# Head of a small language-model layer: four chunks' features share one 128-row operand, and a table repeated in four diagonal blocks multiplies it

## What is computed

```
attempts, correct = running counts per (row, skill)          # (32, 512)
f = [skill, attempts, correct / max(attempts, 1), 1]         # four features per token
h = f @ table                       # (32, 512, 64), table is (4, 64)
v = ln(h); scan over 512 steps: x_t = (0.97 x + relu(v Dx^T)) / its L1 norm
           a = rho x_t; y = relu(ln(a) Dy^T) * relu(x_t); out = ln(y E^T)
           rho = 0.97 rho + ln(v) x_t^T
h = h + out; h = h + top-2-of-8 expert MLP(ln(h))
```

## Time and profile before

| | us |
|---|---|
| median of 3 runs (lowest, highest) | 656.93 (656.39, 657.41) |
| the profiled execution | 657.44 |
| its span, first to last instruction | 655.6 |
| groups of the head in it | 62.7 to 107.7 |
| serial stretch behind them | 107.7 to 128.4 |
| turns | 128.4 to the end |

### The profile page before, as it was taken

The page is one execution under the profiler, slowest core; times in us unless marked ns, Lnnn a source line. Parts: engine busy times, 40 slices in busy tenths (PEclk is TensorE's granted clock), DMA queues, the critical chain, the costliest instruction groups (busy, mean ns, idle before and its releaser), DMA issues.

```text
span 655.6 us, 18935 instructions
## 1 busy us (share of the span) xinstructions
PE 609.0 (93%) x5109; PEld 436.1 (67%) x5109; DVE 530.2 (81%) x1890; ACT 426.3 (65%) x1291; POOL 358.0 (55%) x441
## 2 busy tenths in 40 slices
PE   2484998799999999999999999999999999999997
PEld 0363776466677777777777777777777777777744
DVE  4998878765788888888888888888888888888675
ACT  6892776023567766667777667776666677776683
POOL 3001999414365555565666666655666566555654
PEclk9999998899999999999999999999999999999999
DMA  6300000100444444455455544444444444444364
GB/s 198 135 0 1 1 0 1 40 33 33 98 98 108 106 105 109 119 113 117 110 118 109 117 120 120 106 105 105 105 105 105 105 105 105 106 105 106 83 131 98
DMA packets 61623, 60.43 MB, mean 92 GB/s; under 512 B 22124, under 2 KB 57052, under 8 KB 61084
## 3 DMA queue, kind: packets, MB, share of 16 engines
q1 hardware_dynamic: 59164, 59.36, 37.8%
q10 hardware_dynamic: 2240, 0.73, 0.5%
q0 software_dynamic: 192, 0.01, 0.0%
HBM read 55.20 MB, written 4.89 MB: 92 GB/s over the span
## 4 chain that ended last, share of the span: by engine, by line
PE 87%; DVE 8%; issue 2%; ACT 1%; DMA 1%; SPq 0%; POOL 0%; DVEq 0%; ACTq 0%; POOLq 0%
PE bank L1614 16%; PE bank L1472 11%; PE bank L1595 9%; PE bank L1599 8%; PE bank L1537 5%; PE bank L1558 4%; PE bank L1494 3%; PE bank L1508 3%; PE bank L1513 3%; PE bank L1379 2%; PE bank L1483 2%; PE bank L1370 2%; PE bank L1462 2%; PE bank L1332 2%; PE bank L1361 2%
## 5 line engine op out<-in xcount | busy, mean ns | idle before, releaser
L687 ACT ACTIVATE skill_rows<-bank,b1T,w_scale 128x512 f32<-128x512 f32 x256 | 196.1, 778 | 8.4 <-PE bank L1599 6.6
L520 POOL TENSOR_TENSOR feat_parts<-skill_rows 128x512 f32<-128x512 f32 x62 | 79.0, 1275 | 93.8 <-DVE feat_parts L1047 88.9
L1614 PE MATMUL bank<-skill_rows,w_sb 128*64 128x256 f32 x928 | 122.7, 382 | 0.0
L1472 PE MATMUL bank<-feat_parts 128*128 128x128 f32 (+1 forms) x512 | 88.1, 306 | 2.5 <-DVE feat_parts L1030 1.2
L1614 PEld LDWEIGHTS bank<-skill_rows,w_sb 128*64 128x64 f32 x928 | 69.3, 137 | 27.2
L1472 PEld LDWEIGHTS bank<-feat_parts 128*128 128x128 f32 x512 | 78.1, 194 | 11.8 <-DVE feat_parts L1030 1.6
L1047 DVE TENSOR_TENSOR_SCAN feat_parts<-same,feat_parts 128x512 f32<-128x512 f32 x62 | 72.2, 1207 | 0.0
L1148 DVE SCALAR_TENSOR_TENSOR skill_rows<-bank,b2T,skill_rows 128x256 f32<-128x256 f32 x120 | 51.1, 477 | 16.3 <-PE bank L1614 13.4
L711 ACT ACTIVATE bank<-bank 128x64 f32<-128x64 f32 x128 | 26.7, 220 | 50.9 <-PE bank L1567 50.9
L1053 DVE TENSOR_TENSOR feat_parts<-bank,mask_sb 128x128 f32<-128x128 f32 x128 | 36.3, 285 | 28.6 <-PE bank L1472 27.3
L1148 DVE SCALAR_TENSOR_TENSOR skill_rows<-bank,b2T,feat_parts 128x256 f32<-128x256 f32 x112 | 47.6, 478 | 12.6 <-PE bank L1614 11.3
(11 more groups left out here) (284 smaller groups left out, 1506.8 us busy)
## 6 DMA issues: line engine op xcount, KB each, us to landing
skill_rows<-w_d SPq DMA_DIRECT2D x32, 512.0 KB, 6.3
same<-factor_d SPq DMA_DIRECT2D x31, 512.0 KB, 5.5
feat_parts<-w_d SPq DMA_DIRECT2D x30, 512.0 KB, 6.3
skill_rows<-skill_row_d SPq DMA_DIRECT2D x4, 1024.0 KB, 7.8
out<-o_sb SPq DMA_DIRECT2D x28, 128.0 KB, 5.2
feat_parts<-w_d SPq DMA_DIRECT2D x4, 256.0 KB, 4.9
w_sb<-in_L_ffn_W ACTq DMA_DIRECT2D x2, 256.0 KB
w_d<-wT SPq DMA_DIRECT2D x32, 16.0 KB, 1.4
```

Of the source, the lines that this page charges most:

```text
L520: pool.tensor_tensor(half[:, n, :], tm[:, 2 * n, :], tm[:, 2 * n + 1, :], ALU.add).then_inc(po_half, 1)
L687: act.activation(hid[:, e, :], banks[e % len(banks)][:, :], ACT.Gelu, bias=b1T[:, e:e + 1], scale=w1_scale[:, e:e + 1]).then_inc(ac_gelu, 1)
L1472: last = pe.matmul(n_bank[sc % 2][:, 0:SPAN[sc]], xs[:, k, sc * P:(sc + 1) * P], xs[:, k, sc * P:sc * P + SPAN[sc]], start=(k == 0), stop= ...
L1614: last = pe.matmul(z_bank[q % 2][n * D:(n + 1) * D, at:at + S // 2], w2_sb[:, e, :], hid[:, e, n * (S // 2):(n + 1) * (S // 2)], start=Tru ...
```

## The change

The features now take SLOTS = 8 columns for a piece (4 whole, 2 middle, 2 low) and ROWS = 32 columns for a chunk, so that four chunks fill 128. One transpose gives `feat_k` the rows of four chunks. `table_k` has four diagonal blocks: block c holds the table in rows 32c to 32c+23 and zeros elsewhere. A group is 2 transposes, 2 products of 256 columns and 4 of 512 columns. The zeros, the copies and the transposed features shrink with it; `table_k`, its clearing by VectorE before the counting, and the table's transfers on SyncE's queue (10 before, 13 now) grow.

Banks 2 and 4 are read by ScalarE now, 3 and 5 by VectorE (before 2 and 3, 4 and 5). `h` of even groups is copied by ScalarE, of odd groups by VectorE.

`update(b, k)` has to give each chunk its own weights: four products of 128 columns in place of one of 512.

On GpSimd the quadratic form is written with operations that multiply and add in one, with scalars by partition, in 19 steps up to `rstd` where there were 24 (the first, `gram_two`, on 20 columns in both). The power for `u_scale` is cut in two: 8 columns (rows of tokens 0 and 1) before `weighted_input(0)`, 120 behind it, and the mean comes before both.

```diff
-KF = NF * PIECES * PIECES
+SLOTS = 8
+ROWS = P // C
...
-        table_k = sb("table_k", [P, D + NS], BF16)
+        table_k = sb("table_k", [P, C, D + NS], BF16)
...
+        slots = parts_flat[:, 0:J * ROWS].rearrange("p (j n) -> p j n", n=ROWS)
...
+            for c in range(C):
+                sp.dma_start(table_k[c * ROWS:c * ROWS + PIECES * SLOTS, c, :], table_d.rearrange("g s n -> (g s) n"))\
+                  .then_inc(ld_table, 16)
...
+                def more(total, f, scalar):
+                    step(pool.tensor_scalar(t, f, scalar, None, ALU.mult))
+                    step(pool.tensor_tensor(total, total, t, ALU.add))
...
+                step(pool.tensor_scalar(a, skill, one(0, 0), two(0, 3), ALU.mult, ALU.add))
+                more(a, tries, two(0, 1))
+                more(a, ratio, two(0, 2))
+                step(pool.tensor_tensor(a, a, skill, ALU.mult))
...
             moments()
+            input_scales(0, 2)
             weighted_input(0)
+            input_scales(2, B)
+            pool.wait_ge(scales_in, 2)
...
             def group(g, side):
-                act.wait_ge(pe_h0, g + 1)
-                act.activation(h_all[:, bass.ds(g * GROUP * D, GROUP * D)], h0_bank[side][:, :], ACT.Copy)\
-                   .then_inc(h0_in, 1)
-                for n in range(HALF):
+                if side == 0:
+                    act.wait_ge(pe_h0, g + 1)
+                    act.activation(h_all[:, bass.ds(g * GROUP * D, GROUP * D)], h0_bank[side][:, :], ACT.Copy)\
+                       .then_inc(h0_a, 1)
+                for n in range(0, PAIRS, 2):
...
-                dve.tensor_copy(feat_k[:, bass.ds(g * GROUP * P, GROUP * P)], feat_bank[side][:, :].bitcast(BF16))\
+                dve.tensor_copy(feat_k[:, bass.ds(g * 2 * P, 2 * P)], feat_bank[side][:, :].bitcast(BF16)[:, 0:2 * P])\
                    .then_inc(featT_in, 1)
...
+                if side == 1:
+                    dve.wait_ge(pe_h0, g + 1)
+                    dve.tensor_copy(h_all[:, bass.ds(g * GROUP * D, GROUP * D)], h0_bank[side][:, :]).then_inc(h0_v, 1)
+                for n in range(1, PAIRS, 2):
...
-            def group(g, side):
+            def group(g, side, pair):
                 pe.wait_ge(featT_in, g + 1)
-                wait(pe, h0_in, g - 1)
-                for n in range(GROUP):
-                    last = pe.matmul(h0_bank[side][:, n * D:(n + 1) * D], feat_k[:, bass.ds((g * GROUP + n) * P, P)],
-                                     table_k[:, 0:D], start=True, stop=True)
+                wait(pe, (h0_a, h0_v)[side], pair)
+                for n in range(2):
+                    last = pe.matmul(h0_bank[side][:, n * C * D:(n + 1) * C * D].rearrange("p (c d) -> p c d", c=C),
+                                     feat_k[:, bass.ds((2 * g + n) * P, P)], table_k[:, :, 0:D], start=True, stop=True)
                 last.then_inc(pe_h0, 1)
...
             def update(b, k):
 
                 wait(pe, dv_y, 2 * NK * b + NK * (k - 1))
-                pe.matmul(n_bank[k][:, :], table_k[:, D + k * P:D + (k + 1) * P],
-                          feat_k[:, bass.ds(b * S, S)], start=True, stop=True).then_inc(pe_pre, 1)
+                for c in range(C):
+                    last = pe.matmul(n_bank[k][:, c * P:(c + 1) * P], table_k[:, c, D + k * P:D + (k + 1) * P],
+                                     feat_k[:, bass.ds(b * P, P)], start=True, stop=True)
+                last.then_inc(pe_pre, 1)
```

More of the change, by code:

```diff
@@ L432, in _ @@
             pool.wait_ge(rows_set, 3)
-            def each(row, i, j):
-                at = i * (NF + 1) + j
-                return row[:, at:at + 1].to_broadcast([P, J])
             def moments():
                 k = Steps(pool, form_steps)
-                f, t = [feat[:, i, :] for i in range(NF)], form[:, 3, :]
-                def step(out, a, b, how):
-                    k.done(pool.tensor_tensor(out, a, b, how))
+                skill, tries, ratio, ok = [feat[:, i, :] for i in range(NF)]
@@ L458, in moments @@
[L458 to L464, removed]
-                pool.tensor_tensor(rstd[:], rstd[:], power_j[:], ALU.pow).then_inc(rstd_in, 1)
@@ L466, in moments @@
[L466 to L471, removed]
+                step(pool.tensor_tensor(gram_two[:], gram_row[:], gram_row[:], ALU.add))
@@ new lines, in moments @@
+                step(pool.tensor_scalar(b, ratio, one(2, 2), two(2, 3), ALU.mult, ALU.add))
+                step(pool.tensor_tensor(b, b, ratio, ALU.mult))
+                step(pool.tensor_tensor(a, a, b, ALU.add))
+                more(a, ok, one(3, 3))
+                step(pool.tensor_scalar(var_h0[:], a, 0.0, None, ALU.max))
+                step(pool.tensor_scalar(rstd[:], var_h0[:], EPS, DECAY * DECAY, ALU.add, ALU.mult))
+                pool.tensor_tensor(rstd[:], rstd[:], power_j[:], ALU.pow).then_inc(rstd_in, 1)
@@ L472, in moments @@
                     .then_inc(scales_in, 1)
[L473 to L476, removed]
             def weighted_input(b):
@@ L1372, in group @@
                 last.then_inc(pe_h0, 1)
                 for n in range(PAIRS):
-                    read = 2 * HALF * (g - 1) + 2 * (n % HALF) + 2
                     if not isinstance(g, int) or g > 0:
-                        pe.wait_ge(sum_a if n < HALF else sum_v, read)
-                    for k in range(2):
-                        last = pe.matmul(bank[2 + n][:, k * NS:(k + 1) * NS],
-                                         feat_k[:, bass.ds((g * GROUP + 2 * n + k) * P, P)],
-                                         table_k[:, D:D + NS], start=True, stop=True)
@@ L1412, in keep_running @@
                 for _ in range(n):
-                    pe.matmul(idle_bank[:, :], table_k[:, D:D + P], feat_k[:, 0:S], start=True, stop=True)
+                    pe.matmul(idle_bank[:, :], table_k[:, 0, D:D + P], feat_k[:, 0:S], start=True, stop=True)
             keep_running(2, bank[1])
```

104 lines of the change are left out of this document (61 added, 43 removed).

## The result

| | before | with the change |
|---|---|---|
| median (lowest to highest), 4 runs each | 656.66 us (655.71 to 657.41) | 645.50 us (645.01 to 646.25) |
| ratio of the times, 95% interval | | 0.9834 [0.9815, 0.9852] |
| profiled execution; its span | 657.44; 655.6 us | 645.01; 643.2 us |

The kernel is 11.2 us faster by the medians. In the tables here the span is cut at four marks: the first transpose of the head's groups, VectorE's product of `upd_sum` with `rstd`, the first product with `skill_rows,first` behind the scans, and the first transpose of the turns.

A forecast was written before the change was run, and what follows sets the result against it. TensorE's instruction count was taken to bound the head's groups, and TensorE to fill the main loop. -10.5 (groups) and +0.6 (updates) gave -9.9: 647.0 us against the 656.93 median, range 644.5 to 653.5.

The forecast's parts named there:

- The bound of before: Head's groups: TensorE sets the pace by its count of instructions, with an address row ahead of each, not by columns.
- The groups: Head's groups: VectorE becomes the bound at 4.0 us for two groups; stage ends at 97.2 instead of 107.7, -10.5 us.
- The two unknown copies: VectorE in the head's groups: feature copy of 256 columns taken as 0.25 less 0.05 overlap, copy of `h` as 0.55 us.
- bounds for the stage: VectorE's sums and copies in the head's groups: 31.5 us expected, 30.9 to 37.5 with the bounds of both copies.
- Ahead of the groups: Before the head's groups: clearing `table_k` +0.40 us, two shorter copies of feature columns -0.37 for both.
- The serial stretch: Scans and products behind the head's groups: instructions unchanged, no sum; low-clock parts may fall elsewhere, +-1 us.
- The updates: 64 updates, each four products of 128 columns for one of 512: 0.01 us more each, +0.6 us.
- The rival by which they would cost more: Updates: weight loads only half hidden, 5.1 instead of 0.6 us, 651.5; by the skill's page 653.1; chance 0.08.
- it does not hold `rstd`: GpSimd beside the head's groups: `rstd`'s power starts at 72.5, ends at 93.3, 3.9 us ahead of VectorE.
- 5 us of cover: GpSimd before the turns: second power done at 120.3, `ub` of row 1 wanted at 125.6.
- The lower clock: Rival, head's groups: TensorE at 1.2 GHz needs 4.7 us for two groups, 5.6 more, 652.6; chance 0.07.
- The slower case: Rival, loop of turns: each piece of an update pays 0.14 us, 18 us over 52 updates, 665; chance 0.05.

## Why the prediction was right

The forecast was -9.9 us. The medians give -11.2, the two profiles -12.5 between their spans. Part of both is luck with the clock: all four runs of the change had a mean granted clock of 0.995, while 20 of the 39 later runs of the kernel before had 0.992 or less. At equal clock, over all runs of the two kernels on all chips, the change gives 10.0 us (655.66 and 645.70 at 0.995, 11 and 7 runs) and 10.5 (657.10 and 646.56 at 0.992, 18 and 2 runs). So the sum was nearer than the medians show.

**The bound of before.** The loop's rows for each product, not its columns, set TensorE's pace: shown by the loop written out, whose products are the same and take 0.40 for 1.14 us.

**The groups: forecast -10.5, measured -10.9** (and -10.7 in the second profile of the change). VectorE is the bound, 3.98 us for two groups against a forecast of 4.0, and ScalarE stands close behind it, with 0.2 to 0.35 us of waiting in two groups. The two unknown copies, in the groups by line and shape:

```profile
L951 DVE COPY h_all<-bank 128x512 f32 x6 | 4.1, 684 | 0.0
L945 DVE COPY feat_k<-bank 128x256 bf16 x12 | 3.5, 289 | 0.0
```

The copy of `h` has 684 ns; the row that gave the upper bound had 683. It starts 0.59 us ahead of its neighbour (78.37 to 78.96); forecast 0.55. The copy of 256 columns has 289 ns, 0.21 from start to start; forecast 0.20. The start of the stage, 2.27 us to VectorE's first sum, was forecast as 2.16. The row for the stretch says clock 1.00, but four products of 512 columns take 1.71 us in the chain of the first group and 0.90 in a later one: half the clock at first, as the forecast had it from the earlier trace rows. The forecast's bounds for the stage, "30.9 to 37.5", do not follow from its own terms (64 sums, 14 and 8 copies and 0.8 give 30.9 to 38.8); nothing rested on them.

**Ahead of the groups: forecast +0.03, measured -0.5.** Clearing `table_k` costs +0.41 as worked out. In this profile the transfer ahead of it landed earlier by as much (VectorE's row behind it starts at 6.65 us, 7.12 before), which hid it. What is left is VectorE's copies of feature columns, 0.43 us each for 0.56, and its three casts ahead of them, shorter by 0.2 together, which the sum lacked. The earlier landing is luck: the groups start at 62.1 to 63.0 us in the four profiles of the old layout and at 62.2 to 62.9 in the ten of the new one, so a gain of 0.5 is not shown, and the forecast of nothing stands.

**The serial stretch: forecast 0 (+-1), measured -1.4.** This is the largest difference from the sum in the two profiles. No profile has the stretch under 10.68 us, which in the changed kernel VectorE's own steps fill. The timeline of before has TensorE's transposes of the two sums at 1.06 us for four, and VectorE's first scan waited 1.10 us for them:

```profile
109.05 1.06 PE L1419 MATMUL bank<-ident_f,upd_sum 128*32 128x128 f32 x4
109.90 1.06 PE L1419 MATMUL bank<-ident_f,rstd 128*32 128x128 f32 x4
```

```profile
110.22 1.21 DVE L970 TENSOR_TENSOR_SCAN skill_rows<-bank,skill_rows 32x512 f32<-32x512 f32 x1 [1.10 <-PE bank L1419]
```

The same rows of the changed kernel have 0.60, and no wait; the chain behind the groups runs through VectorE alone:

```profile
97.38 0.60 PE L1438 MATMUL bank<-ident_f,upd_sum 128*32 128x128 f32 x4
97.82 0.60 PE L1438 MATMUL bank<-ident_f,rstd 128*32 128x128 f32 x4
```

```profile
95.15 1.16 DVE bank L957 x6
...
97.37 0.66 DVE w1g L989
...
98.09 1.22 DVE skill_rows L993
...
103.62 3.35 DVE skill_rows L1000
...
107.01 1.12 PE bank L1458 x2
```

The granted clock was 0.57 from 108 to 112, right where before's sums are transposed, and 0.58 from 102 to 106 in the changed kernel, under TensorE's filler work, where nobody waits. The forecast said that these parts "may fall elsewhere" and gave them no sum. Over all profiles here the stretch took 10.7 to 15.0 us, with and without the change: without fillers 10.68, 12.08 and 14.95 in the old layout, and 10.7 to 13.6 in the new one. So the runs do not show that the change shortens it, and the 1.4 are taken as the luck of two executions. The profile of before has the lower clock three times behind the groups (from 108, 115 and 129 us), that of the change twice (from 102 and 116). Executions with a mean clock of 0.992 are 1.4 us slower than those with 0.995 in the kernel before, and 0.9 in the changed one. The forecast's +-1 for this was of the right size.

**The updates: forecast +0.6, measured +0.3** in the turns, and 0.5 by the experiment with one product. The chain of waits in the main loop answers to the earlier trace rows:

```profile
308.64 0.24 PE bank L1482 x4
...
309.40 0.22 PE bank L1482 x4
...
313.84 0.22 PE bank L1598 x4
```

Four products of 128 columns with their weights take 0.24 and 0.22 us, as the transposes of L1598 do: 55 to 60 ns each. The rival by which they would cost more falls, by row and by experiment. With it falls, for these products, the figure of the Trainium skill ("TensorE: Matmul & The Clock Gate", sustained throughput) of about 81 ns for a load and product of 128 columns; the same page's 55.6 ns for products of 128 columns back to back (section "Wait — 56ns, not 53.3ns?") is what the trace agrees with, loads included.

**GpSimd: right that it does not hold `rstd`, wrong on the cover.** The power starts at 72.90 (forecast 72.5) and ends at 93.7 (93.3), 2.6 us ahead of its user. But the prediction gave `ub` of row 1 "5 us of cover", and the timeline leaves 0.34:

```profile
62.65 0.44 POOL L464 TENSOR_SCALAR form<-feat,gram_row,gram_two 128x128 f32<-128x128 f32 x1
63.18 0.61 POOL L458 TENSOR_SCALAR form<-feat,gram_two 128x128 f32<-128x128 f32 x1
...
72.90 20.81 POOL L478 TENSOR_TENSOR rstd<-rstd,power_j 128x128 f32<-128x128 f32 x1
...
97.39 1.11 POOL L458 TENSOR_SCALAR form<-feat,gram_row 128x128 f32<-128x128 f32 x1
...
101.32 1.52 POOL L499 TENSOR_TENSOR same<-h_all,u_scale 128x256 f32<-128x256 f32 x1
102.80 19.51 POOL L487 TENSOR_TENSOR u_scale<-u_scale,power_j 128x120 f32<-128x120 f32 x1
...
123.11 0.61 POOL L499 TENSOR_TENSOR same<-h_all,u_scale 128x256 f32<-128x256 f32 x1 [0.34 <-PE bank L1534]
```

Forecast was that the second power is done at 120.3 and wanted at 125.6 (135.84 less 10.5 is 125.3). It was done at 122.78, 2.5 us later, and wanted at 123.1, 2.5 earlier. The second is the gain of this profile, 12.7 us up to here. The first lies mostly in the step "0.4, the mean 4.1, ... 0.3 and 0.6": one step of the mean took 1.11 us where its equals took 0.60, and `ub` of row 0 took 1.52 where that of row 1 took 0.61, 1.4 together; 0.4 more is the later end of `rstd`'s power. With more than 0.34 us on top, row 1's `ub` would have been late; with the old moments row 0's is, and the kernel is 2.6 us slower.

**The other rivals.** The lower clock did not come back inside the groups once they were under way (L1399 takes 0.90 us for four from 68 us on), though TensorE is busy only 30.3 of 36 us. The slower case needed an address row for each piece of an update; there is none, and a turn is as long as before.

## What to carry to other kernels

In a loop with a counter on TensorE, count the products, not only their columns: here a small product with an address row took 0.14 us, and 0.05 without one. Writing such a loop out is the cheapest trial: one line changed gave 9 of the 11 us by the medians, 8 of 10 at equal clock. Beside the written-out loop the packed operand shortens the groups by 3.1 us more, but the times of the two written-out kernels (0.9866 and 0.9862) do not show it, since the second met the lower clock; with fillers, at a mean clock of 0.995, it has 645.8 us against 647.6. When one engine's stage is cut by 11 us, work out for each engine beside it when its result is wanted *then*, and price its steps with its neighbour at work: cover that looked like 5 us was 0.34. And before a difference of 1 or 2 us is explained, compare executions of equal mean clock.

## What the runs showed of the hardware that was not expected

Some of GpSimd's steps stretch while VectorE works on certain rows. The 1.11 us and the 1.52 us above fall on these two of VectorE:

```profile
97.29 0.74 DVE L989 TENSOR_SCALAR w1g<-w_sb,gam 64x1024 f32<-64x1024 f32 x1
...
101.21 1.21 DVE L997 TENSOR_TENSOR_SCAN skill_rows<-skill_rows 32x512 f32<-32x512 f32 x1
```

One is an operation on 1024 float32 columns, the other a scan with both inputs in SBUF. In the profile of the experiment with the mean moved, `ub` of row 0 at 96.68 took 0.61, and in that of the one product for an update another step of the mean, on two inputs, took 0.96 us for 0.45 beside the same VectorE operation. A scan that reads one of its inputs from a bank (L993, 98.09 to 99.30) left GpSimd's step beside it at 0.45. VectorE pays as well: its `bet_wide` operation took 0.28 us in the kernel before and 0.54 in the changed one, and `w1g` 0.94 for 0.74 with the mean moved. The coincidence is seen, not tested by itself. The Trainium skill ("GPSIMD Engine Reference", Specifications) says that the two engines share their ways to SBUF and collide when VectorE runs a two-port mode or reads two SBUF inputs. The scans agree with the second case (L997 reads two inputs in SBUF, L993 one); whether the operation on 1024 columns runs in such a mode no row here shows.

On GpSimd a scalar step with one operation (0.61 us at 63.18) is dearer than one with two (0.44 at 62.65), both with scalars by partition and 128 columns.

The place where the clock falls behind the groups differs from profile to profile, between 97 and 121 us; in the two profiles of the changed kernel it is near 102 both times. In all four profiles with seven filler products the serial stretch was 10.7 to 11.0 us; without them it was so in five, and 12.1 to 15.0 in the other five. In the changed kernel and in its unrolled form TensorE had waited 1.79 us for VectorE's last sums right ahead, alike in both, and the clock fell at 102 in one and at 98 in the other; so that wait alone does not decide it. What does stays open.
